# A gated cross-attention and expert block: the order of the first rounds rewritten, the expert weights split one round later

## The chip, the cores and the metric

The kernel runs on one core of one Trainium2 chip. The metric is the device time of one execution in microseconds (us). A core has five engines with a program of their own: TensorE (PE, matrix products), VectorE (DVE), ScalarE (ACT), GpSimd (POOL) and SyncE (SP, which issues the transfers). Each works through its instructions in order, and they wait for one another on semaphores.

## The reference

The input is 32 sequences of 128 tokens and 256 channels, each with a context of the same size. Two gated blocks follow one another. Block A is cross-attention with 16 heads of 16 channels, queries from the normalised input, keys and values from the context, with a mask over the keys. Block B is a transformer layer: rotary self-attention with a causal mask, a layer norm, and a mixture of 8 experts of which the two best count for each token.

```python
x = x + tanh(g_xattn[0]) * xattn(_layernorm(x), ctx, ctx, mask, Wq, bq, Wk, bk, Wv, bv, Wo, bo)
x = x + tanh(g_ffn[0])   * ffn(_layernorm(x), ...)
# ffn(x):
q, k = rope(x) @ Wq.T + bq, rope(x) @ Wk.T + bk ; v = x @ Wv.T + bv
x1 = _layer_norm(x + softmax(causal(q k^T) * scale) v @ out_proj_w.T + out_proj_b, ln1_w, ln1_b)
gates = softmax(x1 @ gate_w.T + gate_b)                       # 8 experts, the top 2 are kept
moe = sum over the top 2 of gate_e * (x1 @ expert_w[e].T + expert_b[e])
return _layer_norm(x1 + moe, ln2_w, ln2_b)
```

## The kernel before, in words

One sequence is one **tile** (128 tokens on the partitions, 256 channels), and tiles 2r and 2r+1 form a pair. Each engine has one written-out list of steps, a **round**, that is repeated over r; a step is called with the tile it works on (`scores("A", 2 * r - 1)`) and does nothing when that tile does not exist. So the steps of several tiles are interleaved by hand, and the first rounds hold few of them: the pipeline is filling. ACT's and DVE's round numbers are not those of PE. PE's r = 1 goes with ACT's end of r = 3 and start of r = 4, and with DVE's end of r = 1 and first part of r = 2; the last part of DVE's r = 2 goes with the end of PE's r = 1 and the start of its r = 2.

For one tile the steps of a block's attention form a loop between engines, all on the same four banks of PSUM, the score banks. (1) ACT writes the mask into the banks (`seed_scores`). (2) PE adds the scores (`scores`, L516). (3) DVE takes the maxima of each row, one bank after the other (`maxima`, L1022), and writes the 16 of them negated in two bfloat16 parts (`max_parts`, L1034 and L1036). (4) For block A, ACT writes the transposed mask (`seed_scores_t`, L785), each bank once its maxima are out. (5) PE adds the transposed scores (`scores_t`, L535) and transposes the maxima (`transpose_max`, L546), ACT copies them out (`max_transposed`, L818), and PE subtracts them (`subtract_max`, L556). (6) ACT takes the exponentials (`exponentials`, L826); only then are the banks free for the seeds (L776) of the next tile. The order of the tiles on the banks is A of 2r-1, B of 2r-3, A of 2r, B of 2r-2, so in the first rounds: A0, A1, A2, B0, A3, B1, A4. In block B, POOL then zeroes the probabilities above the diagonal (`causal`, L1343).

Around the loop: `attend` (L574) is the product with the values, `raw_values` its copy (`o_raw`, L834), `normalise` transposes it on PE (L585) and divides by the sums on DVE (L1043, L1051), `o_transposed` turns it back, and `project_o` multiplies by the output weights; DVE's `finish_a` adds the residual (L1060) and gives x1. From x1 follow `statistics("B")`, POOL's reciprocal root, DVE's `apply_y` (L964, yn), POOL's `rope` (L1293 to L1299), PE's `rope_transposed`, and keys and queries of block B for the pair (`project_k_b`, `project_q_b`). `x_t` transposes the normalised input (xn), `project_q_a`, `project_k_a` and `project_v_a` give block A's heads.

All float32 products run as three products of a high and a low part (fp32r). Every operand is therefore copied twice: ACT writes the high part (`high_part`, `high_part_of_pair`), DVE the rest (`low_part`, `low_part_of_pair`). The weights are split so as well, once, one 128x512 piece at a time: ACT's `split_high(m)` (L750) from a staging buffer, then DVE's `split_low(m)` (L933). There are 16 pieces, Ak, Av, Aq, Ao, Bk, Bq, Bv, Bo and the experts E0 to E7, and six staging buffers: SP loads piece n only when the low part of piece n-6 is written. After E7, SP goes on to load tile 6. The first use of the experts is `expert_pair(0, 0)` in PE's r = 3.

`keep_busy(use, t, count)` (L411) lets PE multiply a constant `count` times into a bank that is free, with a result that nobody reads; it stands where PE would else wait in the first and the last rounds. `take_work` adds the waits that protect one of the four other banks, by a fixed table of uses (`WORK_USES`), which the change does not touch.

Of the kernel before, what the change touches and what calls it, by code (L numbers as in the profile page):

```python
# [135 lines left out]
def build(nc, dram, out):  # L136
    tiles = out.shape[0]
    with ExitStack() as ctx:
# [246 lines left out]
        def tensor_program(pe):  # L385
# [241 lines left out]
            for r in rounds:  # L627
                gate(2 * r - 6)
                project_v_b(2 * r - 4)
                if r == 1:  # L630
                    keep_busy("x_t", 2, 3)
# [6 lines left out]
                scores("A", 2 * r - 1)  # L638
# [18 lines left out]
                if r == 1:  # L657
                    keep_busy("A_v", 2, 4)
# [8 lines left out]
                project_k_a(r)  # L667
# [4 lines left out]
                project_v_a(2 * r)  # L672
# [3 lines left out]
                transpose_max("B", 2 * r - 3)  # L676
                o_transposed("A", 2 * r - 1)
                if r == 0:
                    keep_busy("A_max_t", 0, 6)
                x_t(2 * r + 1)  # L680
# [7 lines left out]
                project_q_a(r)  # L688
# [5 lines left out]
                if r == 1:  # L694
                    keep_busy("rope_t", 1, 3)
# [8 lines left out]
                if r == 0:  # L704
                    keep_busy("A_max_t", 0, 13)
                if r == 1:
                    keep_busy("rope_t", 1, 14)
# [3 lines left out]
                transpose_max("A", 2 * r)  # L711
# [26 lines left out]
                if r == 0:  # L738
                    keep_busy("x_t", 2, 5)
# [5 lines left out]
        def scalar_program(act):  # L745
# [112 lines left out]
            for r in rounds:  # L858
                if r == 4:
                    split_high("E6")  # L860
                    split_high("E7")
                seed_scores_t(2 * r - 6)
                raw_values("B", 2 * r - 9)
                if r == 3:
                    split_high("Ao")
                    split_high("Bk")
                    split_high("Bq")
                    split_high("Bv")
                if r == 4:
                    small_parts()  # L870
                max_transposed("A", 2 * r - 6)
                high_part_of_pair("rope_t", rope_t, "rope_t", ("B_q_mm", "B_k_mm"), 2 * r - 7)
# [5 lines left out]
                high_part("u_t", u_t, "u_t", ("e_mm", 4), 2 * r - 10)  # L878
                raw_values("A", 2 * r - 6)
# [593 lines left out]
```

## Time and profile before

| | |
|---|---|
| time before, median of 3 runs | 830.11 us (830.05 to 830.32) |
| the profiled execution's own time | 831.21 us |
| its span, first to last instruction | 829.5 us |
| PE busy | 779.7 us (94%) |
| DVE busy | 667.5 us (80%) |
| ACT busy | 564.4 us (68%) |
| POOL busy | 473.0 us (57%) |
| chain that ended last | PE 56%, ACT 24%, DVE 14% |

Busy time is summed over the whole span, so it hides that the first 120 us look different from the rest. The chain that ended last is followed back from the last instruction: at each step to what released it, or to the instruction before it on its engine. A row of a timeline gives the start, the duration, engine, line and operation, with the names of output and inputs, and in brackets how long the engine sat idle before it and what ended that. Consecutive short instructions of an engine overlap by their latency, so one that is shown with 0.62 us may be followed by the next after 0.52.

### The profile page before, as it was taken

How to read it: one execution, taken by the hardware profiler on the slowest of the kernel's cores; microseconds unless marked ns; L12 is line 12 of the kernel's file. 1: busy time of each engine (PE TensorE's matmuls, PEld its weight loads, DVE VectorE, ACT ScalarE, POOL GpSimd, SP SyncE). 2: the span in 40 equal slices, each digit the busy share in tenths (PEclk: the TensorE clock that was granted, in tenths of full speed). 3: DMA queues.
4: the chain of work that ended last, by engine and by line, in shares of the span. 5: the costliest groups of instructions: out<-in, count | busy, mean ns of one | idle time of the engine just before them, and what ended most of it. 6: DMA issues, size and time to landing. Idle time of an engine off the chain costs nothing.

```text
span 829.5 us, 24325 instructions
## 1 busy us (share of the span) xinstructions
PE 779.7 (94%) x9515; PEld 611.9 (74%) x9515; DVE 667.5 (80%) x1908; ACT 564.4 (68%) x1268; POOL 473.0 (57%) x854
## 2 busy tenths in 40 slices
PE   8888989999999999999999999999999999999896
PEld 4465768777787787778787788778778777777663
DVE  5756668797978979797988979797988979787876
ACT  5786767777786777777776777678677777764320
POOL 8434535566665646566574646566564655555343
PEclk9999999999999999999999999999999999999999
DMA  7510000010100101010100101010010000000000
GB/s 202 159 39 16 2 17 16 8 37 9 37 8 2 37 8 36 9 36 9 29 16 2 38 8 37 8 37 9 10 35 2 9 8 8 9 8 8 8 7 20
DMA packets 33570, 20.75 MB, mean 25 GB/s; under 512 B 11672, under 2 KB 33456, under 8 KB 33456
## 3 DMA queue, kind: packets, MB, share of 16 engines
q1 hardware_dynamic: 33456, 19.19, 8.1%
q8 instruction: 76, 1.25, 0.6%
q14 instruction: 38, 0.31, 0.1%
HBM read 14.99 MB, written 4.19 MB: 23 GB/s over the span
## 4 chain that ended last, share of the span: by engine, by line
PE 56%; ACT 24%; DVE 14%; issue 4%; POOL 1%; DMA 0%; SPq 0%; DVEq 0%; POOLq 0%
PE bank L395 26%; PE bank L516 8%; PE bank L535 7%; ACT bank L776 6%; DVE neg_max_A L1022 6%; ACT bank L785 5%; DVE moe L1131 4%; ACT probs_B L826 3%; PE bank L556 3%; PE bank L585 3%; ACT probs_A L826 3%; PE bank L574 2%; PE bank L404 2%; ACT k_heads_B L809 2%; PE bank L546 1%
## 5 line engine op out<-in xcount | busy, mean ns | idle before, releaser
L1343 POOL TENSOR_SCALAR_AFFINE_SELECT probs_B<-probs_B 128x512 f32<-128x512 f32 x128 | 77.3, 640 | 184.4 <-ACT probs_B L826 184.4
L1131 DVE SCALAR_TENSOR_TENSOR moe<-bank,gates,moe 128x256 f32<-128x256 f32 x256 | 123.2, 481 | 48.2 <-PE bank L395 33.2
L785 ACT ACTIVATE bank<-mask_add 128x512 f32<-128x512 bf16 x128 | 76.6, 602 | 49.2 <-DVE neg_max_A L1022 49.2
L395 PE MATMUL bank<-w_expertsa,u_t_a 128*128 128x512 f32 x256 | 105.6, 413 | 0.1
L395 PE MATMUL bank<-w_expertsa,u_t_b 128*128 128x512 f32 x256 | 100.9, 394 | 0.0
L395 PE MATMUL bank<-w_expertsb,u_t_a 128*128 128x512 f32 x256 | 100.9, 394 | 0.0
L1022 DVE TENSOR_REDUCE neg_max_A<-bank 128x4 f32<-128x512 f32 x128 | 79.5, 684 | 11.9 <-PE bank L516 11.5
L1022 DVE TENSOR_REDUCE neg_max_B<-bank 128x4 f32<-128x512 f32 x128 | 79.3, 682 | 5.5 <-PE bank L516 5.5
L776 ACT ACTIVATE bank<-mask_add 128x512 f32<-128x512 bf16 x128 | 69.8, 626 | 0.0
L776 ACT ACTIVATE bank<-causal_add 128x512 f32<-128x512 bf16 x128 | 69.7, 623 | 0.0
L826 ACT ACTIVATE probs_A<-bank 128x512 f32<-128x512 f32 x128 | 66.1, 603 | 4.4 <-PE bank L556 2.2
L826 ACT ACTIVATE probs_B<-bank 128x512 f32<-128x512 f32 x128 | 66.2, 607 | 3.2 <-PE bank L556 1.1
L834 ACT ACTIVATE o_raw<-bank 128x512 f32<-128x512 f32 x64 | 38.5, 602 | 27.8 <-PE bank L574 27.8
L395 PEld LDWEIGHTS bank<-w_expertsa,u_t_a 128*128 128x128 f32 x256 | 49.1, 192 | 10.6 <-issue 0.4
L1260 POOL TENSOR_SCALAR var_eps<-mean_var 128x1 f32<-128x1 f32 x64 | 12.3, 192 | 77.7 <-DVE mean_var L960 75.2
L395 PEld LDWEIGHTS bank<-w_expertsa,u_t_b 128*128 128x128 f32 x256 | 48.1, 188 | 11.4
L395 PEld LDWEIGHTS bank<-w_expertsb,u_t_a 128*128 128x128 f32 x256 | 48.3, 189 | 6.7
L535 PEld LDWEIGHTS bank<-q_heads_A,k_heads_A 32*128 32x128 f32 x1024 | 31.4, 186 | 22.4 <-ACT bank L785 22.4
L809 ACT ACTIVATE k_heads_A<-bank,k_cols_A,head_rows 128x256 f32<-128x256 f32 x64 | 30.9, 565 | 23.0 <-PE bank L395 23.0
L535 PE MATMUL bank<-q_heads_A,k_heads_A 32*128 32x128 f32 x1024 | 37.5, 283 | 8.1 <-ACT bank L785 7.4
L411 PE MATMUL bank<-ident_bf 128*128 128x512 bf16 x167 | 42.7, 396 | 1.9 <-ACT k_heads_B L809 1.9
L516 PE MATMUL bank<-k_heads_A,q_heads_A 32*128 32x256 f32 x512 | 36.7, 399 | 5.8 <-ACT bank L776 4.7
(224 smaller groups left out, 2440.5 us busy)
## 6 DMA issues: line engine op xcount, KB each, us to landing
x_in<-in_x SPq DMA_DIRECT2D x32, 128.0 KB, 2.2
ctx_t<-in_ctxT SPq DMA_DIRECT2D x32, 128.0 KB, 2.2
out<-y_out SPq DMA_DIRECT2D x32, 128.0 KB, 1.7
w_stage<-in_expertsT SPq DMA_DIRECT2D x8, 256.0 KB, 4.3
mask_u<-in_masks SPq DMA_DIRECT2D x32, 32.0 KB, 2.1
w_stage<-in_in_projT SPq DMA_DIRECT2D x3, 256.0 KB, 4.8
w_stage<-in_WkT SPq DMA_DIRECT2D x1, 256.0 KB, 3.5
w_stage<-in_WvT SPq DMA_DIRECT2D x1, 256.0 KB, 3.6
```

What stands on the lines that cost most here:

```text
L395: done = pe.matmul(out_ap, l, r, start=n == 0, stop=n == len(terms) - 1)
L411: pe.matmul(bank[:], ident_bf[:], ident_bf[:].unsqueeze(1).to_broadcast([P, GROUP, P]), start=True, stop=True)
L516: done = pe.matmul(score_banks[g][:, c * 2 * P:(c + 1) * 2 * P], queries[strip, half, c, :], keys[strip, half, c, :, :], start=False, stop ...
L535: pe.matmul(score_banks[g][:, i * P:(i + 1) * P], keys[strip, half, c, odd, :], queries[strip, half, c, :], start=tag == "B" and i == 0, s ...
L776: act.activation(score_banks[g][:].rearrange("p (h k) -> p h k", k=P), mask[:, 0:1, :].to_broadcast([P, GROUP, P]), ACT.Copy).then_inc(sem ...
L785: act.activation(score_banks[g][:].rearrange("p (h k) -> p h k", k=P), mask_add[t % MASK_SLOTS][:, 1:2, :].to_broadcast([P, GROUP, P]), AC ...
L809: act.activation(k_heads[tag][pair % PAIR_SLOTS][:, :, c, odd, :], bank[:, c * PAIR * P:(c + 1) * PAIR * P].rearrange("p (j n) -> p j n", ...
L826: act.activation(probs[tag][:, g * GROUP:(g + 1) * GROUP, :].rearrange("p h q -> p (h q)"), score_banks[g][:], ACT.Exp, scale=SCALE).then_ ...
L834: act.activation(o_raw[:], work_bank(tag + "_values", t)[:], ACT.Copy).then_inc(sem[tag + "_or"], 1)
L1022: dve.tensor_reduce(neg_max[tag][:, g * GROUP:(g + 1) * GROUP], score_banks[g][:].rearrange("p (h k) -> p h k", k=P), AXIS_X, ALU.max, neg ...
L1131: dve.scalar_tensor_tensor(out=moe[(e + 1) % 2][:], in0=bank[:, (e % 2) * EMBED:(e % 2 + 1) * EMBED], scalar=gates[:, e:e + 1], in1=moe[e ...
L1343: pool.affine_select(out=part, in_=part, compare_op=ALU.is_ge, fill=0.0, base=0, pattern=[[0, GROUP], [1, P]], channel_multiplier=-1).then ...
```

## The change

It touches the lists of the first rounds and nothing behind them; apart from the filler, each product, copy and split that was done is still done once. POOL's first `base_b` gets a wait for loaded rows.

- **PE, r = 0:** `transpose_max("A", 0)` goes ahead of `scores_t("A", 0)`; the filler before it is 14 for 13, and one later filler 4 for 5.
- **PE, r = 1:** `scores("A", 1)` goes ahead of `project_o("A", 0)`; `transpose_max` ahead of `scores_t`; `project_k_a(1)` ahead of `attend("A", 1)`; `project_v_a(2)` and `x_t(3)` ahead of `normalise("A", 1)`; `rope_transposed(0)` from before `subtract_max("A", 1)` to before `o_transposed("A", 1)`; `project_q_a(1)` ahead of `project_o("A", 1)`. The filler is cut into other portions, 54 for 52.
- **ACT:** `seed_scores("A", 1)` goes ahead of the copy of tile 0's output; Ao and Bk are split behind `max_transposed("A", 0)`, Bv and Bo after the seeds; of the experts, E0 and E1 now stand before tile 2's transposed seeds, E2 before tile 2's `raw_values`, E3 between `max_transposed("B", 0)` and the copy of tile 2's output, E4 and E5 between the exponentials of B0 and the seeds of A3, E6 and E7 before the transposed seeds of A3.
- **DVE:** maxima and `max_parts` of A1 go ahead of `finish_a(0)`, the maxima of A2 ahead of `apply_y(1)`; the low parts of E0 and E1 stand between the maxima of B0 and its `max_parts`, E2 and E3 a few steps later, E4 and E5 right before the maxima of A3, E6 and E7 behind its `max_parts`.

```diff
 # PE
                 if r == 1:
-                    keep_busy("x_t", 2, 3)
+                    keep_busy("x_t", 2, 2)
+                if r == 1:
+                    scores("A", 2 * r - 1)
                 project_o("A", 2 * r - 2)
...
                 if r == 1:
-                    keep_busy("A_v", 2, 15)
+                    keep_busy("A_v", 2, 10)
...
+                if r == 1:
+                    transpose_max("A", 2 * r - 1)
                 scores_t("A", 2 * r - 1)
-                transpose_max("A", 2 * r - 1)
-                rope_transposed(2 * r - 2)
...
                 if r == 1:
-                    keep_busy("A_v", 2, 4)
+                    keep_busy("A_v", 2, 3)
+                if r == 1:
+                    project_k_a(r)
                 attend("A", 2 * r - 1)
...
+                if r == 1:
+                    keep_busy("A_v", 2, 3)
+                if r == 1:
+                    project_v_a(2 * r)
+                if r == 1:
+                    x_t(2 * r + 1)
                 normalise("A", 2 * r - 1)
...
+                if r == 1:
+                    keep_busy("rope_t", 0, 3)
+                if r == 1:
+                    rope_transposed(2 * r - 2)
                 o_transposed("A", 2 * r - 1)
...
                 if r == 1:
-                    keep_busy("rope_t", 1, 5)
+                    keep_busy("A_values", 2, 3)
+                if r == 1:
+                    project_q_a(r)
                 project_o("A", 2 * r - 1)
...
                 if r == 1:
-                    keep_busy("rope_t", 1, 3)
+                    keep_busy("A_values", 2, 8)
...
                 scores("A", 2 * r)
...
+                if r == 0:
+                    transpose_max("A", 2 * r)
                 scores_t("A", 2 * r)
...
 # ACT
                 if r == 4:
-                    split_high("E6")
-                    split_high("E7")
+                    split_high("E0")
+                    split_high("E1")
                 seed_scores_t(2 * r - 6)
...
                 max_transposed("B", 2 * r - 8)
+                if r == 4:
+                    split_high("E3")
                 if r == 3:
-                    split_high("Bo")
+                    seed_scores("A", 2 * r - 5)
                 high_part("A_o_t", o_t["A"], "A_ot", ("A_o_mm", 1), 2 * r - 6)
                 exponentials("B", 2 * r - 8)
-                seed_scores("A", 2 * r - 5)
+                if r == 4:
+                    split_high("E4")
+                    split_high("E5")
+                if r != 3:
+                    seed_scores("A", 2 * r - 5)
...
 # DVE
                 statistics("A", 2 * r + 1)
                 add_values("B", 2 * r - 5)
+                if r == 2:
+                    maxima("A", 2 * r - 2)
                 apply_y(2 * r - 3)
...
                 add_values("A", 2 * r - 1)
+                if r == 2:
+                    split_low("E0")
+                    split_low("E1")
                 inverse_sums("A", 2 * r - 2)
                 max_parts("B", 2 * r - 4)
...
                 apply_y(2 * r - 2)
+                if r == 2:
+                    split_low("E4")
+                    split_low("E5")
+                if r != 1:
+                    maxima("A", 2 * r - 1)
...
 # POOL
                 if t >= 1:
                     pool.wait_ge(sem["B_res"], t)
+                else:
+                    pool.wait_ge(sem["ld_rows"], 16 * 10)
                 pool.tensor_tensor(base["B"][:], yn[t % Y_SLOTS][:], rows["bo_B"][:], ALU.add).then_inc(sem["B_base"], 1)
```

## Rows read from the trace of the kernel before

**Rows 1.** Page, part 1: busy time of the engines.

```profile
PE 779.7 (94%) x9515; PEld 611.9 (74%) x9515; DVE 667.5 (80%) x1908; ACT 564.4 (68%) x1268; POOL 473.0 (57%) x854
```

**Rows 2.** Busy time in two stretches, window us then engines in order, clock, DMA.

```profile
69.60:74.00 4.40, 3.24 (x57) 2.33 (x55) 2.26 (x6) 4.11 (x9) 3.79 (x8) 1.00 0.00 0
150.00:170.00 20.00, 19.54 (x239) 16.45 (x238) 15.54 (x49) 14.16 (x34) 8.64 (x17) 1.00 0.03 9
```

**Rows 3.** Chain of waits that ended last, 25 to 125 us: start, us, what.

```profile
46.44 2.41 PE bank L395 x18
...
56.24 2.06 ACT probs_A L826 x4
...
68.82 0.64 ACT probs_B L826 x2
...
70.88 2.05 ACT bank L776 x4
...
73.06 1.15 PE bank L516 x16
```

**Rows 4.** Timeline of PE, 0 to 32 us: start, us, what, [idle before].

```profile
3.95 2.77 PE L411 MATMUL bank<-ident_bf 128*128 128x512 bf16 x6
...
22.79 0.40 PE L556 MATMUL bank<-neg_max_t_A,pick 32*128 32x128 bf16 x16 [0.94 <-ACT neg_max_t_A L818]
...
28.27 0.27 PE L404 MATMUL bank<-ident,o_norm_A 128*128 128x128 f32 x1
...
31.27 1.15 PE L516 MATMUL bank<-k_heads_A,q_heads_A 32*128 32x256 f32 x16 [0.38 <-ACT bank L776]
```

**Rows 5.** Timeline of ACT, 28 to 39 us.

```profile
28.97 2.15 ACT L776 ACTIVATE bank<-mask_add 128x512 f32<-128x512 bf16 x4
...
38.44 2.06 ACT L826 ACTIVATE probs_A<-bank 128x512 f32<-128x512 f32 x4 [0.15 <-PE bank L556]
```

**Rows 6.** Timeline of DVE, 33 us: tile 1's maxima.

```profile
33.14 2.48 DVE L1022 TENSOR_REDUCE neg_max_A<-bank 128x4 f32<-128x512 f32 x4
```

**Rows 7.** Timeline of PE, 49 to 65 us.

```profile
49.76 1.15 PE L516 MATMUL bank<-k_heads_A,q_heads_A 32*128 32x256 f32 x16 [0.27 <-ACT q_heads_A L795]
50.84 3.20 PE L411 MATMUL bank<-ident_bf 128*128 128x512 bf16 x14
...
55.27 0.28 PE L404 MATMUL bank<-ident,roped 128*128 128x128 f32 x1
...
64.05 1.08 PE L574 MATMUL bank<-probs_A,values_A 128*32 128x128 f32 x32
```

**Rows 8.** Timeline of ACT, 48 to 51 us.

```profile
48.87 0.84 ACT L795 ACTIVATE q_heads_A<-bank,bias_cols 128x256 f32<-128x256 f32 x2 [0.95 <-PE bank L395]
49.60 1.15 ACT L750 ACTIVATE w_expertsa<-w_stage 128x512 fp32r<-128x512 f32 x2
```

**Rows 9.** Timeline of POOL, 75 us: last step of a rope.

```profile
75.89 0.73 POOL L1299 TENSOR_TENSOR roped<-roped,rope_tmp 128x256 f32<-128x256 f32 x1
```

**Rows 10.** Timeline of DVE, 36 to 75 us.

```profile
36.90 2.82 DVE L933 TENSOR_TENSOR w_expertsb<-w_stage,w_expertsa 128x512 fp32r<-128x512 f32 x3
...
41.05 1.29 DVE L933 TENSOR_TENSOR w_expertsb<-w_stage,w_expertsa 128x512 fp32r<-128x512 f32 x2 [0.35 <-ACT w_expertsa L750]
...
67.20 0.23 DVE L1036 TENSOR_TENSOR neg_max_bf_B<-neg_max_B,neg_max_bf_B 128x64 bf16<-128x64 f32 x1
...
73.59 0.40 DVE L964 TENSOR_SCALAR yn<-x,mean_var_B,rstd_B 128x256 f32<-128x256 f32 x1
74.19 2.48 DVE L1022 TENSOR_REDUCE neg_max_A<-bank 128x4 f32<-128x512 f32 x4 [0.20 <-PE bank L516]
```

**Rows 11.** Timeline of PE, 67 us.

```profile
67.78 0.23 PE L546 MATMUL bank<-ident_bf,neg_max_bf_B 128*128 128x128 bf16 x1
```

**Rows 12.** Timeline of POOL, 77 us: tile 6 context.

```profile
77.92 0.40 POOL L1271 CAST ctx_ab_a<-ctx_t 128x256 fp32r<-128x256 f32 x1
```

**Rows 13.** Timeline of PE, 107 us: filler behind a wait.

```profile
107.14 1.47 PE L411 MATMUL bank<-ident_bf 128*128 128x512 bf16 x6 [1.88 <-ACT k_heads_B L809]
```

More of the change, by code:

```diff
@@ L637, in tensor_program @@
                 attend("B", 2 * r - 4)
-                scores("A", 2 * r - 1)
+                if r != 1:
+                    scores("A", 2 * r - 1)
                 if r == 18:
@@ L679, in tensor_program @@
                     keep_busy("A_max_t", 0, 6)
-                x_t(2 * r + 1)
+                if r != 1:
+                    x_t(2 * r + 1)
                 subtract_max("B", 2 * r - 3)
@@ L687, in tensor_program @@
                     keep_busy("A_max_t", 0, 4)
-                project_q_a(r)
+                if r != 1:
+                    project_q_a(r)
                 project_v_b(2 * r - 3)
@@ L738, in tensor_program @@
                 if r == 0:
-                    keep_busy("x_t", 2, 5)
+                    keep_busy("x_t", 2, 4)
                 o_transposed("A", 2 * r)
@@ L1153, in vector_program @@
                 expert_sum(6, 2 * r - 8)
+                if r == 2:
+                    split_low("Bo")
                 apply_x(2 * r - 1)
@@ L1162, in vector_program @@
                 if r == 2:
-                    split_low("E3")
-                    split_low("E4")
+                    add_values("A", 2 * r - 2)
                 inverse_sums("A", 2 * r - 3)
@@ L1189, in vector_program @@
                 gates_low(2 * r - 7)
-                maxima("A", 2 * r - 2)
+                if r != 2:
+                    maxima("A", 2 * r - 2)
                 bias_sum(2 * r - 7)
@@ L1196, in vector_program @@
                 expert_sum(3, 2 * r - 7)
-                if r == 2:
-                    split_low("E6")
-                    split_low("E7")
                 low_part_of_pair("rope_t", rope_t, "rope_t", 2 * r - 3)
@@ L1225, in vector_program @@
                 mean_variance("A", 2 * r + 1)
-                if r == 1:
-                    split_low("Bo")
+                if r == 2:
+                    split_low("E2")
                 low_part("A_o_t", o_t["A"], "A_ot", 2 * r - 2)
@@ L1230, in vector_program @@
                 add_values("B", 2 * r - 4)
+                if r == 1:
+                    split_low("Bv")
+                if r == 2:
+                    split_low("E3")
+                if r == 1:
+                    maxima("A", 2 * r - 1)
+                if r == 1:
+                    max_parts("A", 2 * r - 1)
                 finish_a(2 * r - 2)
@@ L1244, in vector_program @@
                 apply_y(2 * r - 2)
-                maxima("A", 2 * r - 1)
+                if r == 2:
+                    split_low("E4")
+                    split_low("E5")
+                if r != 1:
+                    maxima("A", 2 * r - 1)
                 bias_sum(2 * r - 6)
@@ L1248, in vector_program @@
                 expert_sum(1, 2 * r - 6)
-                max_parts("A", 2 * r - 1)
+                if r != 1:
+                    max_parts("A", 2 * r - 1)
                 expert_sum(2, 2 * r - 6)
+                if r == 2:
+                    split_low("E6")
+                    split_low("E7")
                 apply_u(2 * r - 5)
```

68 lines of the change are left out of this document (38 added, 30 removed).

## The prediction

> **What bounds the kernel now.** I read the page first: PE is busy for 94% of the span, no other engine for over 80% [rows 1]. Then busy time by stretch: behind 150 us PE works 19.54 of 20 us, but between 69.6 and 74 us only 3.24 of 4.40 [rows 2], and part of the work of the first 110 us is filler. So there are two stages. Behind some 110 us PE sets the pace; in front of that a loop does, and the third view, the chain of waits, names its members: ACT's exponentials, ACT's seeds, PE's scores, DVE's maxima, round again [rows 3]. The change touches that loop alone. Whatever moves the start of the full stage moves the end by as much, since PE leaves 0.5 us in 20 idle there, too little to swallow a delay or to give more. The forecast is thus a difference at one point, the maxima of tile A3 (74.19 us before), the last place where a moved step stands on the loop. Such a difference holds for any execution: the profiled one took 831.21 us, 829.5 of it span (the table), 1.1 above the median of 830.11, and I add the difference to the median.
>
> **Tile A0.** PE waits 0.94 us for ACT's copy of the transposed maxima [rows 4]; ACT is still splitting four weights, and the transpose stands behind `scores_t`. With the transpose first and two of the splits gone both are off the path. The 14th filler ends before the maxima are out. Exponentials and all behind them come 1.0 us earlier, `o_transposed` at 27.2 for 28.27 [rows 4].
>
> **Tile A1.** Before, ACT's seeds stand behind the copy of tile 0's output, at 28.97, and the scores start at 31.27, after `project_o` and `x_t` [rows 4, 5]. Now the seeds follow `o_raw` at 25.6, last 2.15 and end at 27.75: scores at 27.9, which is 3.4 us earlier. DVE's maxima, held at 33.14 by tile 0's residual and statistics [rows 6], start when bank and Bv's split let them, at 29.2: 3.9 earlier. The exponentials stood 5.3 behind the maxima (38.44 - 33.14) [rows 5, 6]; now the parts of the maxima are taken while POOL is quiet and their transpose is out earlier, so 5.0: 34.2 for 38.44, gain 4.2.
>
> **From there to the scores of A2** I walk PE's list. Subtraction and 3 fillers to 34.8, keys (12 products at 0.13, 18 take 2.41 [rows 3]) to 36.2, `attend` (1.08 [rows 7], all exponentials there) to 37.2, 3 fillers to 37.9, `project_v_a` to 38.6; the values (0.4, and 0.3 to get there) free the bank at 39.3, `x_t(3)` and `normalise` to 40.0, DVE's two divisions at 41.0, both transposes to 41.3, ACT's three copies in a row to 42.1, DVE's part of xn at 42.6. `project_q_a` starts at 42.7 and its heads are out 2.5 later (46.44 + 0.7 of `project_o` = 47.2; queries 48.87 + 0.84 = 49.7) [rows 3, 8]: 45.2. But PE still has `project_o` and 8 fillers: 3.20 us for 14 is 0.23 each [rows 7], 44.2 + 0.7 + 1.8 = 46.6. So **filler, not data, starts the scores of A2** at 46.6 for 49.76, gain 3.2. If I err by a few tenths there, the 1.3 us of overhang absorbs it.
>
> **A new wait in A2.** `apply_y(1)` moves behind the maxima. Before, the rope's transpose lay 5.5 behind the scores and found its input ready. Now: 1.2 to the maxima, 2.5 for them, 0.4 for yn, 2.6 for the rope (yn 73.59 to the rope's end 75.89 + 0.73, less yn's own 0.40) [rows 9, 10]: 6.7, at 53.3 for 55.27 [rows 7]. Behind the transpose in PE's queue stand the subtraction and B0's keys. The exponentials of A2 start at 53.95 for 56.24: **2.3 us are left** of 3.2. From there to B0's maxima nothing on the path changes; E2's copy falls into ACT's wait for `attend`.
>
> **The expert splits** are what takes it back; four pieces of it, in times of before.
> 1. *E0, E1 low, on DVE between B0's maxima and `max_parts`.* Two such took 1.29, the next instruction being free after 1.20 [rows 10]. The negated parts ended at 67.43 (67.20 + 0.23), the transpose stood at 67.78 [rows 10, 11]: slack 0.3, so 0.9 lands on the path.
> 2. *E3 high on ACT*, 0.52 ahead of the exponentials of B0; a small gap there covers half: 0.3.
> 3. *E4, E5 high on ACT between the exponentials of B0 and A3's seeds*, which now follow each other (the chain goes 68.82, 70.88, 73.06) [rows 3]. Two such take 1.15, 1.04 to the next one [rows 8]: 1.0. PE then waits for the seeds some 1.5 longer, as `attend` B0 was done half a us before.
> 4. *E4, E5 low on DVE right before A3's maxima.* These wait 0.20 for PE now, behind yn [rows 10]. x_t(4)'s low part and yn shift with the seeds by 2.2; then the two splits, 1.2 us alone [rows 10], end 0.9 after the bank is ready. But here POOL starts the rope in the same moment, and three splits beside POOL's work took 2.82, 0.94 each [rows 10]: then 1.6. I take 1.3.
> Together 0.9 + 0.3 + 1.0 + 1.3 = 3.5, bounds 3.1 and 3.8. In 2, 3 and 4 the cover of before (ACT's and DVE's waits between 31 and 55 us) is what the pieces have lost.
>
> On 4 the Trainium skill ("SBUF — State Buffer", the section on SBUF's two separate sides) says more than the row: a DVE operation with two SBUF inputs, as `split_low` is, and a GpSimd operation that reads SBUF hold the shared port pair in turn, each for its whole length. By that rule, an estimate, both splits could wait for a rope step of 0.73, 2.7 in all, and the sum would be 0.8 us more; the 0.94 of three splits speak for less.
>
> **Everything else** costs nothing, by these covers: E2's and E3's low parts fall into DVE's waits for ACT's and PE's copies; E6, E7 high into ACT's wait for A3's maxima, low into DVE's wait for the rope's copy (1.3 us, so 0.2 may be lost if POOL runs beside). `small_parts` stands in a wait of ACT. POOL's added wait is for rows that landed 40 us before. On SP, E4 and E5 load once Bv and Bo are split (36 us), E6 and E7 only after E0 and E1 low, at 65 us in place of 37, and tiles 6 and 7 queue behind them until 67; a load lands in 2 to 5 us and POOL takes tile 6's context at 77.92 [rows 12]: 5 us to spare. PE's filler, 2 more in r = 1, is in the walk.
>
> **The sum:** -2.3 + 3.5 = +1.2 us, 831.3 for the median. With the bounds of the splits +0.8 to +1.5; if the filler did not bind in A2 and the rope's wait went, up to 1.2 less, and if my walk misses a wait of the kind it cannot see, 1 us more: this case's own range is 829.9 to 832.6.
>
> **Rivals.**
> *The gain survives.* If the four pieces found cover (the splits early enough in ACT's and DVE's queues that bank or POOL still decide), the 2.3 us, or 3.2 with yn early, stay: 827.8, at best 826.9. For it: the pieces only fill waits in tile B0 and E2. Against: the chain runs through ACT from exponentials to seeds without a gap [rows 3] and DVE has 0.2 us ahead of A3's maxima [rows 10].
> *The granted clock falls* (slower). PE works 3.24 of 4.40 us in the stretch of B0 and the seeds [rows 2], at a clock of 1.00 (2.4 GHz). The splits stretch it by 2.2 us without adding work, and 1 to 1.5 us of waiting follows behind 13 fillers. If the clock goes to 1.2 GHz there, fillers cost what the first six did, 2.77 us or 0.46 each [rows 4], for 0.23: 13 of them plus the scores add 3.5, of which 1.3 lie in the wait, and the next products 0.5 or more: +3 on top, 834.3. It decides if that stretch alone is enough; before, PE once idled 1.88 us [rows 13] and the clock held. The skill ("TensorE: Matmul & The Clock Gate", on how the gate oscillates in real kernels) has idle gaps of PE as the cause of such drops, so it speaks against a change that opens them.
> *The sums cancel:* a faster stage one (scores of A2 at 45.4) or uncontended splits give 830.1 to 830.6; that is inside the main case.
>
> **Chances.** Main case 0.72, the gain survives 0.16, the clock falls 0.12. A difference of 0.2% (1.7 us) is about what can be told from none. Of the main case three tenths lie above 831.8, hardly anything below 828.4. Faster by over 0.2%: 0.16 + 0.02 = 0.18. Slower: 0.22 + 0.12 = 0.34. Within: 0.48. The range goes from the surviving gain, 827.6, to 833.4, and leaves out the worse part of the clock case and little else.
>
> **What would show each step.** In the changed trace: A1's scores near 27.9 and its exponentials near 34.2; A2's scores right behind the last of 8 fillers, no wait ahead of them; `rope_transposed(1)` with a wait for POOL of about 1 us; B0's exponentials 1.2 us later behind A2's (12.6 us before [rows 3]); ACT's E4, E5 on the chain ahead of A3's seeds, and PE idle some 2 us before A3's scores; A3's maxima near 75.4 for 74.19. I am wrong if A3's maxima start before 73.5, or if a load is what a split waits for, or if the clock's row is under 1.00 anywhere in 60 to 110 us.

## The result, and the profile after

The changed kernel takes **831.46 us** (median of 18 runs, 830.48 to 833.96) against 830.05 for the kernel before in the same series (18 runs): 1.0019 times the time, with a 95% interval of 1.0012 to 1.0026. It is 1.4 us slower, a little less than the 0.2% that the prediction called the bound between "no change" and "slower". The profiled execution took 831.91 us, with a span of 830.1.

The page says nearly nothing about it (its part 1):

```profile
span 830.1 us, 24329 instructions
...
PE 780.0 (94%) x9517; PEld 611.9 (74%) x9517; DVE 665.5 (80%) x1908; ACT 564.0 (68%) x1268; POOL 472.7 (57%) x854
```

PE is busy for 0.3 us more than in [rows 1] and has two instructions more, the added filler; DVE and ACT do the same work (busy 2.0 and 0.4 us less). All the difference lies in when things start. Two stages again, columns as in [rows 2]:

```profile
69.60:74.00 4.40, 2.23 (x42) 1.50 (x44) 1.79 (x6) 4.40 (x10) 3.40 (x7) 0.89 0.55 143
150.00:170.00 20.00, 19.38 (x252) 16.16 (x250) 15.43 (x49) 14.92 (x35) 8.78 (x17) 1.00 0.03 9
```

In the full stage PE works as before. In the stretch of tile B0 it works 2.23 of 4.40 us where it worked 3.24, and the granted clock of that stretch is 0.89. To see where the time goes I follow one operation, the scores (L516 on PE), through both traces. The first column is the kernel before, the shift is start after minus start before:

| scores of | before, us | after, us | shift |
|---|---|---|---|
| A0 | 16.19 | 16.09 | -0.10 |
| A1 | 31.27 | 27.98 | -3.29 |
| A2 | 49.76 | 46.86 | -2.90 |
| B0 | 62.97 | 61.04 | -1.93 |
| A3 | 73.06 | 73.26 | +0.20 |
| B1 | 83.75 | 85.39 | +1.64 |
| A4 | 94.65 | 96.29 | +1.64 |
| B28 (the 60th) | 744.13 | 745.79 | +1.66 |
| the next B tile | 765.45 | 766.03 | +0.58 |

Three things stand in this table. The new order gains up to 3.3 us. Between B0 and B1 3.6 us are lost. Then the shift of 1.64 is carried through 660 us within 0.1 us (it lies between 1.63 and 1.72 at every tile), as the full stage neither gives nor takes. The last row is about the one execution of the kernel before that was profiled: the granted clock fell in its drain and not in this one's; more on that below. So the difference of the two spans (0.6 us) understates the change, and the medians, 1.4 apart, are the better measure.

PE in the first stage of the changed kernel (start, duration, what, idle time before and what ended it), against [rows 4, 7, 11]:

```profile
20.66 0.23 PE L546 MATMUL bank<-ident_bf,neg_max_bf_A 128*128 128x128 bf16 x1 [0.29 <-DVE neg_max_bf_A L1071]
...
27.98 1.15 PE L516 MATMUL bank<-k_heads_A,q_heads_A 32*128 32x256 f32 x16
...
45.03 1.90 PE L411 MATMUL bank<-ident_bf 128*128 128x512 bf16 x8
46.86 1.15 PE L516 MATMUL bank<-k_heads_A,q_heads_A 32*128 32x256 f32 x16
...
53.49 0.33 PE L404 MATMUL bank<-ident,roped 128*128 128x128 f32 x1 [0.96 <-POOL roped L1354]
...
73.26 2.09 PE L516 MATMUL bank<-k_heads_A,q_heads_A 32*128 32x256 f32 x16 [1.06 <-ACT bank L804]
75.28 3.54 PE L411 MATMUL bank<-ident_bf 128*128 128x512 bf16 x13
```

The scores of A2 start behind the last of 8 fillers with no wait of their own. `rope_transposed(1)` waits 0.96 us for POOL, where [rows 7] had none. The scores of A3 wait 1.06 us for their seeds and then take 2.09 us for the 1.15 of [rows 3]; the 13 fillers behind them take 3.54.

The chain of waits from B0's maxima to A3's (start, duration, what), against [rows 3]:

```profile
65.02 1.20 DVE w_expertsb L968 x2
...
67.29 0.52 ACT w_expertsa L778
...
68.09 0.54 ACT probs_B L854 x2
...
68.93 1.11 ACT probs_B L854 x2
70.04 1.04 ACT w_expertsa L778 x2
71.08 2.04 ACT bank L804 x4
...
74.19 1.74 DVE w_expertsb L968 x2
75.93 0.61 DVE neg_max_A L1057
```

In [rows 3] ACT's seeds (L776) follow its exponentials at once and PE's scores follow the seeds. Here all four pieces of the expert splits stand on the chain itself: 1.20 us of DVE at 65.02, 0.52 and 1.04 of ACT at 67.29 and 70.04, and 1.74 of DVE at 74.19. PE's scores of A3 are no longer on it at all; DVE reaches the maxima later than the bank is ready.

### The profile page after: what moved, and what is told of

It is laid out like the page before. It is cut to its first block, busy times and chain, and to the rows that moved or that the text cites. A ratio compares the mean times of both kernels' runs of the same rounds, so it can differ in the third digit from the quotient of the medians.

```text
span 830.1 us, 24329 instructions
## 1 busy us (share of the span) xinstructions
PE 780.0 (94%) x9517; PEld 611.9 (74%) x9517; DVE 665.5 (80%) x1908; ACT 564.0 (68%) x1268; POOL 472.7 (57%) x854
## 4 chain that ended last, share of the span: by engine, by line
PE 54%; ACT 25%; DVE 15%; issue 4%; POOL 1%; DVEq 0%; POOLq 0%
PE bank L395 23%; PE bank L516 8%; ACT bank L804 7%; PE bank L535 7%; DVE neg_max_A L1057 6%; ACT bank L813 5%; ACT probs_A L854 4%; DVE moe L1166 4%; ACT probs_B L854 3%; PE bank L585 3%; PE bank L556 3%; ACT k_heads_B L837 2%; PE bank L574 2%; PE bank L411 2%; PE bank L404 2%
## 5 line engine op out<-in xcount | busy, mean ns | idle before, releaser
L854 ACT ACTIVATE probs_B<-bank 128x512 f32<-128x512 f32 x128 | 66.2, 607 | 2.9 <-PE bank L556 1.0
L411 PE MATMUL bank<-ident_bf 128*128 128x512 bf16 x169 | 44.6, 403 | 1.9 <-ACT k_heads_B L837 1.9
L516 PE MATMUL bank<-k_heads_A,q_heads_A 32*128 32x256 f32 x512 | 37.6, 408 | 5.7 <-ACT bank L804 5.0
```

The source lines that it names most:

```text
L411: pe.matmul(bank[:], ident_bf[:], ident_bf[:].unsqueeze(1).to_broadcast([P, GROUP, P]), start=True, stop=True)
L516: done = pe.matmul(score_banks[g][:, c * 2 * P:(c + 1) * 2 * P], queries[strip, half, c, :], keys[strip, half, c, :, :], start=False, stop ...
L854: act.activation(probs[tag][:, g * GROUP:(g + 1) * GROUP, :].rearrange("p h q -> p (h q)"), score_banks[g][:], ACT.Exp, scale=SCALE).then_ ...
```

## The experiments

All of these runs were timed beside the kernel before on the same chip; the ratio is to that. It is taken over the whole series, so it can differ by up to 0.1% from the quotient of the two medians given in the text. From each profile I read the same points. **Intervals in us, from the start of one operation to the start of another** (scores: L516 on PE, exponentials: ACT, maxima: DVE), which leaves out that tile 0's loads land up to 1.3 us later in some executions:

| kernel | A0 to A2 | A2 to exp. A2 | A2 to B0 | B0 to A3 | A3 to its maxima | A3 to B1 | ratio (95%) |
|---|---|---|---|---|---|---|---|
| before | 33.57 | 6.47 | 13.21 | 10.09 | 1.13 | 10.69 | 1 |
| changed | 30.77 | 7.43 | 14.18 | 12.22 | 2.59 | 12.13 | 1.0019 (1.0012 to 1.0026) |
| x1 splits covered | 30.96 | 8.15 | 15.25 | 10.09 | 1.14 | 10.69 | 0.9994 (0.9985 to 1.0003) |
| x2 late splits only | 32.98 | 6.47 | 13.21 | 12.22 | 2.60 | 14.57 | 1.0045 (1.0032 to 1.0058) |
| x3 yn first | 30.67 | 6.46 | 13.21 | 12.22 | 2.59 | 12.13 | 1.0015 (1.0006 to 1.0023) |
| x4 one filler | 28.94 | 7.47 | 14.20 | 12.22 | 2.59 | 14.57 | 1.0013 (1.0002 to 1.0023) |
| x5 low later | 30.62 | 7.43 | 14.52 | 12.22 | 1.13 | 10.69 | 1.0009 (0.9999 to 1.0020) |
| x6 high covered | 30.66 | 7.42 | 14.17 | 11.09 | 2.60 | 12.14 | 1.0010 (1.0001 to 1.0018) |
| x7 clock kept | 30.88 | 7.43 | 14.17 | 12.27 | 2.54 | 12.08 | 1.0026 (1.0016 to 1.0037) |
| x9 all covered | 29.18 | 7.81 | 14.54 | 10.09 | 1.13 | 10.68 | 0.9969 (0.9959 to 0.9979) |
| x10 yn between | 29.66 | 6.79 | 13.53 | 10.08 | 1.14 | 10.69 | 0.9947 (0.9933 to 0.9961) |
| x11 transpose first | 33.56 | 6.46 | 13.20 | 10.08 | 1.14 | 10.69 | 0.9993 (0.9983 to 1.0003) |
| x12 pieces 2 to 4 out | 30.65 | 7.42 | 14.15 | 11.09 | 1.16 | 10.71 | 0.9992 (0.9983 to 1.0002) |

From A2 on the intervals repeat to a few hundredths between kernels that do not differ there, so they tell causes apart that single runs, which scatter by over 1 us, and the medians cannot. One exception is a fall of the granted clock, which can come in one execution and not in another: A2 to B0 of x5 is 14.52 for 14.18 by one (0.66 from 55 to 60 us).

The first column is coarser. The seven kernels with the order and the filler of the change have 30.62 to 30.96 us there, and the difference lies before A1: DVE's two small operations that write A0's negated maxima (L1069 and L1071 of the changed kernel) took 0.83 us together in the changed kernel, 0.99 in x1 and 0.46 in x4, and PE's transpose and the exponentials of A0 follow them. In the kernel before the same two took 0.69 us, in x2 0.93, and the exponentials came 7.03 and 7.04 us behind the scores: there ACT's splits hide it. From A1's scores to A2's those seven have 18.87 to 18.92 us, x4 17.43, x9 and x10 17.59, x2 17.90, the kernel before 18.49.

**The two halves of the change, each alone.** x2 is the kernel before with POOL's added wait and the expert splits (and `small_parts`) moved to the places of the change, whose `split` lines it takes over as they stand in the diff ahead of the prediction; x1 is the changed kernel with the splits moved to idle time.

```diff
 # x1, ACT
                 if r == 4:
                     split_high("E0")
                     split_high("E1")
+                    split_high("E2")
+                    split_high("E3")
                 seed_scores_t(2 * r - 6)
...
+                if r == 4:
+                    split_high("E4")
+                    split_high("E5")
                 max_transposed("A", 2 * r - 6)
...
                 if r == 4:
-                    split_high("E2")
+                    split_high("E6")
+                    split_high("E7")
                 raw_values("A", 2 * r - 6)
 # x1, DVE (all other expert splits of r = 2 removed)
+                if r == 2:
+                    split_low("E0")
+                    split_low("E1")
                 low_part_of_pair("rope_t", rope_t, "rope_t", 2 * r - 3)
+                if r == 2:
+                    split_low("E2")
+                    split_low("E3")
+                    split_low("E4")
+                    split_low("E5")
...
                 mean_variance("B", 2 * r - 2)
+                if r == 2:
+                    split_low("E6")
+                    split_low("E7")
```

> The changed kernel with its new order kept and only the eight expert splits moved into idle time that its own trace shows: high parts of E0 to E3 before tile 2's transposed seeds, E4 and E5 before its max_transposed, E6 and E7 before its raw_values; low parts of E0 to E5 around tile 1's rope copy, E6 and E7 behind B0's mean_variance. My theory (the new order gains some 2 us up to B0's scores, the four pieces of the splits on the loop take it back and more): scores of B0 stay at 61.0, those of A3 come at 71.1 for 73.06 before and B1 at 81.8 for 83.75; median 828.1, 1.9 under the kernel before and 3.3 under the changed one. Rival (the new order itself costs, the splits are innocent): A3 stays at 73.2, B1 at 85.4, median 831.4.

> The kernel before with its order kept and only the expert splits moved to where the change has them. My theory: without E5's split ahead of tile 1's output the scores of A2 come 0.5 us earlier, 49.3 (5 fillers then decide), then the four pieces cost 3.5: scores of B1 at 86.8 for 83.75, median 833.1. Rival (the splits cost nothing, the order does): B1 at 83.3, median 829.6. Second rival (the pieces cost only together with the new order): B1 within 0.5 of 83.75.

x2 measured 833.14 us against 829.04, ratio 1.0045: the forecast of 833.1 with the kernel before at 830.1 would be 3.0 more, it was 4.1 by the medians and 3.7 by the ratio. The intervals say why. A0 to A2 is 0.59 shorter (forecast 0.5). B0 to A3 grows by 2.13 us (12.22 for 10.09) and A3's maxima come 1.47 later (2.60 for 1.13), as in the changed kernel; so the pieces cost the same with either order. The 2.44 us that A3 to B1 has more than in the changed kernel (14.57 for 12.13) are the granted clock, below, in the execution that was profiled. The one run of x2 with a mean clock of 0.998 took 831.77, 2.9 over the lowest cluster of the kernel before (828.8 to 828.9).

x1 shows the counterpart: both intervals are back at 10.09 and 10.69. But its median is that of the kernel before (829.26 and 829.04), not 1.9 under it. The forecast missed what happens earlier, A2 to B0 is 15.25. The timeline of PE in x1 has this row for `rope_transposed(1)`, where the changed kernel has the one at 53.49 above:

```profile
54.35 0.33 PE L404 MATMUL bank<-ident,roped 128*128 128x128 f32 x1 [1.69 <-POOL roped L1350]
```

And its window of 55 to 60 us (columns as in [rows 2]):

```profile
55.00:60.00 5.00, 4.40 (x35) 4.28 (x24) 3.45 (x5) 5.00 (x11) 1.87 (x3) 0.66 0.77 210
```

PE waits 1.69 us for the rope where the changed kernel waited 0.96, since DVE's splits of E0 and E1 now run beside POOL's rope. That is 0.72 of the 1.07 us that A2 to B0 grew; the rest goes with the clock of 0.66 from 55 to 60 us, as x5 has 0.34 more there with the same clock and the old wait. So moving a split out of one engine's path put it into another's, through the rope.

**The pieces one by one.** x5 takes only the low parts of E4 to E7 away from A3's maxima (behind `apply_x(5)`), x6 only the high parts of E3 to E5 (ahead of `max_transposed("B", 0)`), x12 is both.

```diff
 # x5, DVE (the splits of E4 to E7 in r = 2 removed)
                 apply_x(2 * r - 1)
+                if r == 3:
+                    split_low("E4")
+                    split_low("E5")
+                    split_low("E6")
+                    split_low("E7")
 # x6, ACT
+                if r == 4:
+                    split_high("E3")
+                    split_high("E4")
+                    split_high("E5")
                 max_transposed("B", 2 * r - 8)
-                if r == 4:
-                    split_high("E3")
...
-                if r == 4:
-                    split_high("E4")
-                    split_high("E5")
```

> The changed kernel with the low parts of E4 to E7 taken from around A3's maxima and put behind apply_x(5), where DVE idles 2.5 us. In the changed trace PE's clock row is 0.50 from 73 to 76 us and A3's scores take 2.09 us for 1.15. Theory 1 (DVE's splits alone hold the maxima, the clock is harmless): the maxima start at 74.4 for 75.85, B1's scores at 84.0 for 85.39, the median 1.4 under the changed kernel. Theory 2 (the low clock lies hidden under the splits and comes out when they go): maxima at 75.1, the 13 fillers end at 78.6 whatever happens, B1's scores at 84.9 to 85.1, the median 0.3 to 0.6 lower.

> The changed kernel with the high parts of E3, E4 and E5 on ACT ahead of max_transposed(B, 0), where ACT idles 3.2 us; DVE unchanged. Pieces 2 and 3 of the prediction go: the seeds of A3 start 1.3 earlier against B0's scores (9.9 to 8.6 us behind them), PE no longer waits over a us for them, and the clock row stays at 1.00 from 70 to 80 us. Maxima of A3 at 74.6, still behind E4 and E5 low; B1 at 84.1 for 85.39; median 1.3 under the changed kernel, and fewer of its runs at the upper end. Rival (the loop is held by DVE alone): B1 stays at 85.4.

> x5_low_later and x6_high345_covered together: of the four pieces only the first is left (E0 and E1 low ahead of B0's max_parts). If the pieces add up: B0 to A3 11.1 us between the scores (10.1 before, 12.2 changed), A3 to B1 10.7 as before; B1's scores at 82.8 for 85.39, median 2.5 under the changed kernel, which is 1.0 under the kernel before. Rival (they overlap, one hides the other): B1 at 84.0 or later.

x5: the maxima follow the scores by 1.13 us again and B1 comes 1.44 us sooner; that is piece 4, and DVE's row is gone from the chain. Theory 1 stands for it; theory 2 was not tried in this profile, as the clock did not fall there in that execution (it fell at 55 to 60 us, 0.66). x6: B0 to A3 falls by 1.13, not 1.3. Its median, 830.70 us for 830.02 (ratio 1.0010), cannot be told from the changed kernel's. Its chain of waits (start, duration, what) shows what took over:

```profile
65.43 1.20 DVE w_expertsb L967 x2
...
67.10 0.34 DVE o_norm_A L1085
...
67.49 0.33 PE bank L404
...
67.97 0.38 ACT o_t_A_a L784
68.35 0.59 ACT probs_B L854 x2
```

ACT's exponentials now wait for the copy of tile 2's output, which waits for DVE's o_norm behind E0 and E1: the first piece holds the path a second way. x12 confirms that the rest adds up: 11.09 and 10.71 in one kernel, so of the 3.57 us between B0 and B1 (2.13 + 1.44) 2.55 are pieces 2 to 4 and 1.0 is piece 1. By its points B1 lies 66.60 us behind A0's scores, 1.0 under the kernel before's 67.56; the median moves less, 829.64 for 830.06 with an interval that holds no change. The rival of overlap falls.

**The order's own parts.** x3 puts `apply_y(1)` back ahead of A2's maxima; x4 has 1 filler for 8 ahead of A2's scores; x11 is the kernel before with PE's transpose first for tile A0 and nothing else.

```diff
 # x3, DVE
+                apply_y(2 * r - 3)
                 if r == 2:
                     maxima("A", 2 * r - 2)
-                apply_y(2 * r - 3)
 # x4, PE
                 if r == 1:
-                    keep_busy("A_values", 2, 8)
+                    keep_busy("A_values", 2, 1)
 # x7, PE of the changed kernel (below)
                 attend("B", 2 * r - 4)
+                if r == 2:
+                    keep_busy("A_v", 4, 5)
 # x11, PE of the kernel before
-                    keep_busy("A_max_t", 0, 13)
+                    keep_busy("A_max_t", 0, 14)
+                if r == 0:
+                    transpose_max("A", 2 * r)
                 scores_t("A", 2 * r)
-                transpose_max("A", 2 * r)
+                if r != 0:
+                    transpose_max("A", 2 * r)
```

> The changed kernel with one step back in place: apply_y(1) ahead of the maxima of A2. My theory: the rope is ready at 50 us, PE's wait of 0.96 us before rope_transposed(1) goes, the exponentials of A2 start at 53.3 for 54.3 and the scores of B1 come 1.0 earlier, 84.4; median 830.5. Rival (the wait is hidden behind something else, such as the copy of the maxima, or the gain is eaten by a later wait): B1 at 85.4, median 831.4.

> The changed kernel with 1 filler for 8 between project_o(A, 1) and the scores of A2. My theory (filler, not data, starts these scores): they start at 45.5 for 46.86, right behind the query heads, and all that follows moves by 1.3 to 1.4: scores of B1 at 84.0, median 830.1. Rival (the heads are only just in time): A2's scores move by under 0.3, median 831.3. Second rival: PE idles more, the granted clock falls in 45 to 55 us and takes the gain back.

> The kernel before with PE's part of the change for tile A0 alone: transpose_max ahead of scores_t, 14 fillers for 13 and 4 for 5; ACT's four splits stay ahead of the copy of the maxima. My prediction took 1.0 us for transpose and splits together. Theory: ACT is busy with the splits until 22.5 us, so PE's order alone gives nothing: exponentials of A0 at 23.2, scores of A1 at 31.3, median within 0.2 of the kernel before. Rival (PE's order is the whole gain): exponentials at 22.3, median 0.9 lower.

x3: the exponentials of A2 follow its scores by 6.46 us for 7.43, PE's wait for the rope is gone, and from A0's to B1's scores it is 68.23 us for 69.30. The absolute times in the expectation did not come, since tile 0 itself started 1.3 us late in that profile (17.42 for 16.09). The median fell by less than forecast (ratio 1.0015 for 1.0019, which their 95% intervals do not tell apart). x4: A2's scores come 1.83 us sooner, but 0.38 of that stands before A1 already (DVE's two operations, 0.46 us for 0.83), which the filler cannot touch. From A1's to A2's scores it is 17.43 for 18.88: the seven fillers were worth 1.45 us, as forecast (1.3 to 1.4). The gain reaches A3 undiminished. Behind A3 it is lost in the profiled execution, 14.57 for 12.13, to the clock; five of the 12 runs took 829.25 to 829.59 us, and the other seven 830.49 to 832.47. The second rival, a clock that falls in 45 to 55 us, did not come: those rows are at 1.00. x11: nothing moves, the exponentials of A0 come 7.03 us behind its scores as before, for 6.14 in the changed kernel. So for A0 the order on PE alone is worth nothing; the gain needs ACT's splits behind the copy. Whether it needs the order on PE too was not run.

**The clock.** x7 (its edit stands above) is the changed kernel with 5 fillers in PE's wait for A3's seeds.

> The changed kernel with 5 fillers more, in PE's wait for A3's seeds. The clock row should stay at 1.00 from 70 to 80 us and A3's scores take 1.15 us. Theory 2 (the clock is hidden by DVE's splits in that place): maxima of A3 still at 75.85, B1 at 85.4 in the profile; the median falls only by what the clock costs in the runs in which it falls later, 0 to 0.7 us. Theory 3 (the clock is a term of its own): B1 at 84.6 or earlier, median 0.8 or more lower.

The busy time by window, columns as in [rows 2] (the granted clock is the third number from the end), of the changed kernel:

```profile
73.00:74.00 1.00, 0.74 (x8) 0.72 (x12) 0.55 (x2) 1.00 (x4) 0.33 (x1) 0.52 0.46 106
...
75.00:76.00 1.00, 1.00 (x6) 0.28 (x3) 1.00 (x2) 0.00 (x0) 1.00 (x2) 0.50 0.00 0
...
77.00:78.00 1.00, 1.00 (x6) 0.42 (x5) 1.00 (x3) 1.00 (x3) 1.00 (x2) 1.00 0.00 0
```

Of x7:

```profile
70.00:75.00 5.00, 3.94 (x56) 2.13 (x57) 2.39 (x7) 5.00 (x11) 3.72 (x8) 1.00 0.43 115
75.00:80.00 5.00, 3.36 (x40) 1.80 (x42) 4.93 (x8) 2.93 (x7) 4.78 (x8) 1.00 0.00 0
```

Of x4:

```profile
75.00:80.00 5.00, 3.16 (x58) 2.15 (x55) 4.59 (x8) 3.80 (x10) 4.35 (x6) 0.91 0.22 59
80.00:85.00 5.00, 4.19 (x40) 2.38 (x40) 1.92 (x6) 4.36 (x10) 0.00 (x0) 0.50 0.02 3
85.00:90.00 5.00, 5.00 (x45) 3.67 (x47) 3.07 (x8) 1.48 (x4) 0.00 (x0) 0.91 0.00 0
```

In the changed kernel the clock is at its lower level (0.50, 1.2 GHz) from about 73 to 76.5 us, behind a stretch in which PE worked 2.09 of the 4 us from 69 to 73 with no single wait over 1.06 us. In x7 it stays at 1.00. And yet A3 to B1 is 12.08 us for 12.13, and the median is not lower (1.0026): at that place the low clock lies under DVE's splits and costs nothing, theory 2. x6, with the clock at 1.00 and piece 4 in place, says the same (12.14).

That the fillers kept the clock is not shown by x7's profile at this place. The waits before A3's scores are the same in the changed kernel, x3, x2, x4 and x5 (0.67 to 0.69, 0.44 and 1.05 to 1.06 us), and the clock fell there in the first two and not in the other three. In x4 and x2 it falls some 8 us behind A3's scores instead, after a further wait of 1.69 us behind the 13 fillers; in x4 from 79 to 86 us, with A3's subtraction, the transposes and the products with the values under it. There it costs 2.44 us both times.

**A version that beats both.** x9 has x3's and x4's edits together (2 fillers) and covered splits, E0's low part ahead of `apply_y(1)` and E1's just ahead of `low_part_of_pair`; the others stand as in x1.

```diff
 # x9, DVE
                 if r == 2:
-                    maxima("A", 2 * r - 2)
+                    split_low("E0")
                 apply_y(2 * r - 3)
+                if r == 2:
+                    maxima("A", 2 * r - 2)
...
                 expert_sum(3, 2 * r - 7)
+                if r == 2:
+                    split_low("E1")
                 low_part_of_pair("rope_t", rope_t, "rope_t", 2 * r - 3)
```

> The changed kernel's order with all four losses taken out: apply_y(1) ahead of A2's maxima, 2 fillers for 8 ahead of A2's scores, and the expert splits in idle time as in x1_splits_covered, but E0's low part ahead of apply_y(1) and E1's behind max_parts, since both beside the rope's POOL work delayed the rope in x1_splits_covered from 53.5 to 54.4. My theory: A2's scores at 45.5, its exponentials at 51.9, B0 at 58.7, A3 at 68.8, B1 at 79.5 for 83.75 before; median 4.2 under the kernel before, 824.8 on a chip where that takes 829.0. Rival (PE has too little work in between, the granted clock falls and takes 1 to 3 us back): clock rows under 1.00 in 50 to 80 us, median 826 to 828.

It measured 827.39 us for 830.02, 2.6 us less, where 4.2 were forecast. The rival did not come: every row of the clock between 45 and 95 us is at 1.00. A2 to its exponentials was 7.81 us, 1.3 more than in x3. The timeline of DVE in x9 there (start, duration, line, what, idle time before):

```profile
47.67 0.67 DVE L966 TENSOR_TENSOR w_expertsb<-w_stage,w_expertsa 128x512 fp32r<-128x512 f32 x1
48.79 0.41 DVE L997 TENSOR_SCALAR yn<-x,mean_var_B,rstd_B 128x256 f32<-128x256 f32 x1 [0.44 <-POOL rstd_B L1315]
49.12 2.48 DVE L1055 TENSOR_REDUCE neg_max_A<-bank 128x4 f32<-128x512 f32 x4
```

And of POOL:

```profile
47.79 0.96 POOL L1315 TENSOR_TENSOR rstd_B<-var_eps_B,neg_half 128x1 f32<-128x1 f32 x1
...
49.11 0.55 POOL L1315 TENSOR_TENSOR rstd_A<-var_eps_A,neg_half 128x1 f32<-128x1 f32 x1
```

The split of E0 meets POOL's power for yn, which takes 0.96 us for the 0.55 of the same operation 1.3 us later (and 0.55 in the mean of its 32 in the kernel before); yn waits for it and the maxima, ready at 47.8, wait behind yn. x10 therefore puts yn between the halves of the maxima and both splits behind them.

```diff
 # x10, DVE; splits as in x1, 2 fillers for 8
                 if r == 2:
-                    maxima("A", 2 * r - 2)
+                    maxima("A", 2 * r - 2, (0, 1))
                 apply_y(2 * r - 3)
+                if r == 2:
+                    maxima("A", 2 * r - 2, (2, 3))
```

> x9_all_covered lost 1.3 us of what was expected between A2's scores and B0's, in the trace because apply_y(1) waited for POOL's reciprocal root (slowed to 0.96 us by E0's split beside it) and DVE's maxima behind it started 1.3 after the bank was ready. Here apply_y(1) stands between the second and the third bank's maxima of A2, and E0 and E1 low come behind max_parts; the rest as there. My theory: the exponentials of A2 come 35.8 to 36.0 us behind the scores of A0 (40.05 before, 38.26 changed, 37.0 in x9), B1's scores 63.4 behind them (67.6 before); median 4.0 under the kernel before. Rival (E0 and E1 low now meet the rope on POOL and delay it, as in x1_splits_covered): a wait of POOL before rope_transposed(1), 0.5 to 1 us lost, median 3.0 to 3.5 under it.

Measured: 826.31 us (5 runs, 825.26 to 826.64) for 830.06, ratio 0.9947, interval 0.9933 to 0.9961; 3.8 us off by the medians and 4.4 by the ratio, forecast 4.0. The exponentials of A2 come 36.45 us behind A0's scores, 0.5 late against the forecast, B1's scores 63.96 (63.4). No wait for POOL is left. Its chain in the stretch where the changed kernel lost:

```profile
52.53 2.06 ACT probs_A L854 x4
...
59.26 1.18 PE bank L516 x16
60.44 2.47 DVE neg_max_B L1055 x4
...
65.10 0.64 ACT probs_B L854 x2
...
67.16 2.05 ACT bank L804 x4
...
69.34 1.15 PE bank L516 x16
```

ACT's exponentials, seeds and PE's scores follow each other again as in [rows 3].

## Why the prediction was right

The forecast was 831.3 us in the series in which the kernel before takes 830.1, "no change" likeliest with "slower" behind it; measured 831.46. That the two lie 0.2 us apart is in part luck: at the point of the sum the trace shows +1.66 us for the +1.2 of the text, and the 95% interval of the measured ratio goes from 1.0 to 2.2 us. The sum was made of the right terms:

- *Tile A0, 1.0 us:* the exponentials start at 22.23 where 22.2 follows from the text, 6.14 us behind the scores for 7.03. With the same edit it is 5.76 in x4 and 6.32 in x10, by those two operations of DVE. x11 adds that PE's order alone gives none of it.
- *Tile A1:* scores forecast at 27.9, measured 27.98; exponentials 34.2 and 34.18.
- *Filler starts the scores of A2:* forecast 46.6, measured 46.86, and x4 shows that it is the filler: without seven of the eight, A1's to A2's scores are 1.45 us shorter, near the 1.3 of overhang in the text.
- *The new wait for the rope:* forecast 53.3, measured 53.49 with a wait of 0.96 us (about 1). x3 takes it away for 1.0 us. At B0's scores the gain was 1.93 where I had 2.3; the 0.3 to 0.4 are the filler's and the rope's few tenths.
- *The four pieces, 3.5 us:* pieces 1 to 3 forecast 2.2, measured 2.13; piece 4 forecast 1.3, measured 1.44 (x5). The split into 1, 2 and 3 is less clean than I wrote: with 2 and 3 gone 1.13 us come back, as o_norm behind piece 1 then holds the copy of tile 2's output. The sign named for piece 3, PE idle some 2 us before A3's scores, came as 1.06 us: `attend` of B0, which the text had done early, itself waited 0.67 and 0.44 us for POOL.
- *The port on piece 4:* two splits beside the rope took 1.74 to the next instruction, and POOL's steps 1.11 and 1.43 us for the usual 0.73 and 0.98. The timelines of DVE and POOL in the changed kernel:

```profile
74.11 1.82 DVE L968 TENSOR_TENSOR w_expertsb<-w_stage,w_expertsa 128x512 fp32r<-128x512 f32 x2
```

```profile
74.28 1.11 POOL L1348 TENSOR_TENSOR roped<-yn,rope_cos 128x256 f32<-128x256 f32 x1 [0.94 <-DVE yn L999]
75.34 1.43 POOL L1350 TENSOR_TENSOR rope_tmp<-yn,rope_sin 128x128 f32<-128x128 f32 x2
```

  0.87 per split lies between the 0.60 and 0.94 of [rows 10]. The Trainium skill ("SBUF — State Buffer", on SBUF's two separate sides) has the pair of ports held for a whole instruction by one engine while the other blocks. The trace agrees: read one by one, the first split (74.11) started ahead of POOL's step and took 0.69 us, the second (74.71) took 1.22. So one split waited, where my estimate by that rule, 2.7 us for the two, had both wait. (Its "0.8 us more" counts from the 1.6 of the row; from the 1.3 that I took it would be 1.1.)
- *The point of the sum:* A3's maxima start at 75.85, 1.66 behind the 74.19 of before, where the text had 75.4 and 1.2. The difference of 0.46 is the 2.3 that was 1.9 and a tenth more on the pieces. The lower end of this case's own range should read 829.7 (830.1 + 0.8 - 1.2), not 829.9.
- *The transfers:* SP held the loads of E6 and E7 until DVE's E0 and E1 as forecast (the last was issued at 66.2 us), and no split waited for one.

**What was half wrong is the clock.** The text said that it would be wrong if the clock's row went under 1.00 between 60 and 110 us; it did (0.89 in 69.6 to 74). The rival priced this at 3 us and 12%. It was likelier than that: in the profiles of the changed kernel, x2, x3 and x4 the clock fell between 70 and 90 us. And it can be cheaper: in the profile of the changed kernel it happened and cost nothing, since A3's maxima were waiting for DVE. Where no such cover stands, it costs 2.4 us (x2, x4), near the price. The trace agrees with the Trainium skill ("TensorE: Matmul & The Clock Gate", on how the gate oscillates in real kernels) in that PE waited ahead of the drop; no single wait there was longer than 1.06 us. That these waits alone decide is not shown, as the same waits went by without a drop in x2, x4 and x5.

**The rival "the gain survives"** had 16% and fell: its condition, cover for the pieces, was not met. x10 shows that this cover exists, in other places.

## What to carry to other kernels

While a pipeline fills, a loop through several engines sets the pace, and an instruction that used to fill an engine's wait costs its full length as soon as it stands between two members of that loop. Before a piece of set-up work is moved, find the engine's idle row at the new place in the trace; if there is none, its duration is the price. An idle row is not enough either: in x1 and x9 the splits stood in idle time of DVE and slowed POOL, for which the loop then waited. And filler has a price too: seven fillers of 0.23 us cost 1.45 us on the path here.

## What the runs showed of the hardware

- **The granted clock can fall behind several short waits, and behind the same waits it may not.** In the changed kernel it went to 0.50 after waits of 0.67, 0.44 and 1.06 us and stayed there about 3.5 us, in which PE worked nearly without a pause; x2, x4 and x5 had the same waits and 1.00. Whether a fall costs anything depends on the place: 0 at A3's scores under DVE's splits, 2.44 us where it came 8 us later.
- **Equal kernels differ by the clock in the drain.** The profiled execution of the kernel before, and not that of the changed one, has this (busy time by window, columns as in [rows 2]):

```profile
745.00:750.00 5.00, 3.55 (x51) 2.81 (x43) 4.79 (x18) 0.71 (x3) 0.00 (x0) 0.81 0.00 0
750.00:755.00 5.00, 5.00 (x45) 3.97 (x44) 3.08 (x11) 2.73 (x6) 3.16 (x6) 0.85 0.01 3
```

  Across it the shift between the two traces falls from 1.66 to 0.58 us, so the drop cost 1.1 there. The runs of the kernel before lie in groups about 1.1 us apart (7 of 23 at 828.8 to 828.9, 8 at 829.8 to 830.5, 8 at 831.0 to 831.6), with mean clocks near 0.998, 0.996 and 0.994. That each group is one more such drop is argued from these numbers, not shown. Falls of the clock are a likely reason why a gain of 1 us that the intervals show to 0.05 us (x3, x12) hardly shows in a median.
- **A 128x1 power on POOL took 0.96 us beside one split of DVE**, for the usual 0.55 (x9), though it reads almost nothing. DVE's two operations of 128x64 on A0's maxima took 0.46 us together in x4, 0.83 in the changed kernel and 0.99 in x1, with POOL's steps at other times beside them; that POOL is the cause is not shown.
